# Where the keys of the second attention are split and stacked, in a two-layer gated kernel

## What is computed

```python
# layer 0, attention: 16 heads of 8 channels
q, k, v = Wq @ norm(x) + bq, Wk @ c + bk, Wv @ c + bv
x = x + tanh(g0) * (Wo @ softmax(q k / sqrt(8)) v + bo)
# layer 0, experts: sigmoid gate, 4 of 32 experts (groups of 4, 4 of 8 groups), up -> relu^2 -> down, and a shared one
# layer 1, attention: 8 heads of 16 channels, without projections: q = norm(x), k = v = c
x = x + tanh(g1) * gamma * (softmax(q k / sqrt(16)) v)
# layer 1, experts: softmax gate, 2 of 8 experts, silu(gate) * up -> down, and a shared one
```

## Time and profile before

| what | value |
|---|---|
| median of 3 runs | 777.53 us (777.05 to 778.8) |
| the profiled execution | 779.62 us |
| its span in the profile | 777.4 us |
| TensorE busy | 667.8 us (86%) |
| VectorE busy | 531.6 us (68%) |
| ScalarE busy | 379.0 us (49%) |
| GpSimd busy | 324.1 us (42%) |
| mean granted clock of TensorE | 0.955 |

### The profile page before, as it was taken

The page is one execution under the profiler, slowest core; times in us unless marked ns, Lnnn a source line. Parts: engine busy times, 40 slices in busy tenths (PEclk is TensorE's granted clock), DMA queues, the critical chain, the costliest instruction groups (busy, mean ns, idle before and its releaser), DMA issues.

```text
span 777.4 us, 13620 instructions
## 1 busy us (share of the span) xinstructions
PE 667.8 (86%) x4737; PEld 349.5 (45%) x4738; DVE 531.6 (68%) x1252; ACT 379.0 (49%) x630; POOL 324.1 (42%) x337
## 2 busy tenths in 40 slices
PE   3889999999999899688735788999977999888996
PEld 1233333333333367576402244444433476555763
DVE  3889888888895699155278899997736743222336
ACT  2057888878787344244314566676502213333320
POOL 3535353535011101753568878831100057666530
PEclk9999999999999999889956999999979999999999
DMA  6834343444311800446447778896530022222137
GB/s 164 176 92 122 97 113 96 135 140 130 106 33 38 265 13 2 121 138 184 125 116 190 185 185 205 209 217 158 140 110 28 1 57 83 72 75 66 56 97 258
DMA packets 106362, 93.23 MB, mean 120 GB/s; under 512 B 25205, under 2 KB 92954, under 8 KB 106104
## 3 DMA queue, kind: packets, MB, share of 16 engines
q1 hardware_dynamic: 93600, 67.67, 32.5%
q0 software_dynamic: 8352, 18.74, 8.9%
q10 hardware_dynamic: 4344, 5.97, 2.9%
HBM read 50.63 MB, written 16.01 MB: 86 GB/s over the span
## 4 chain that ended last, share of the span: by engine, by line
PE 56%; DVE 13%; issue 11%; POOL 9%; DMA 4%; ACT 2%; SPq 2%; another core or an unknown queue 1%; ACTq 0%; POOLq 0%; DVEq 0%
PE O L447 9%; PE S L404 9%; PE ST L1547 6%; POOL spare L268 6%; DVE mx L566 4%; PE ST L1473 2%; PE S L1564 2%; PE M L1564 2%; PE ST L943 2%; POOL QKc L279 2%; PE ST L412 2%; PE M L496 2%; DMA QS<-mxT 2%; SPq L165 2%; PE M L489 1%
## 5 line engine op out<-in xcount | busy, mean ns | idle before, releaser
L566 DVE TENSOR_REDUCE mx<-S 128x2 f32<-128x512 f32 x384 | 250.7, 684 | 35.8 <-PE S L404 33.9
L319 ACT ACTIVATE PX<-ST 128x1024 f32<-128x1024 f32 x192 | 195.8, 1022 | 88.2 <-PE ST L412 79.2
L404 PE MATMUL S<-QS 62*128 62x256 bf16 (+1 forms) x768 | 151.2, 292 | 41.6 <-DVE mx L566 28.4
L412 PE MATMUL ST<-QS 64*128 64x256 bf16 (+1 forms) x768 | 141.0, 278 | 7.3 <-DMA QS<-mxT 7.3
L447 PE MATMUL O<-PX,VA 128*32 128x256 f32 x1536 | 123.3, 394 | 0.1
L404 PEld LDWEIGHTS S<-QS 62*128 62x128 bf16 (+1 forms) x768 | 48.7, 97 | 158.2 <-DVE mx L566 95.7
L268 POOL DMA_INDIRECT spare<-ye,GI x64 | 68.9, 1077 | 30.4 <-DMA ye<-QKc 16.1
L1658 POOL DMA_INDIRECT PX<-xn,TI x39 | 39.9, 1022 | 63.4 <-DVE K1n L1847 39.7
L412 PEld LDWEIGHTS ST<-QS 64*128 64x128 bf16 (+1 forms) x768 | 53.4, 96 | 23.3 <-DMA QS<-mxT 9.8
L1547 PE MATMUL ST<-EGU,Cb 128*128 x156 | 54.2, 471 | 6.3 <-ACT Cb L1615 4.9
L786 POOL DMA_INDIRECT PX<-xn,TI x32 | 33.5, 1046 | 61.2 <-DVE spare L1183 44.1
(11 more groups left out here) (302 smaller groups left out, 1114.2 us busy)
## 6 DMA issues: line engine op xcount, KB each, us to landing
QS<-QKs SPq DMA_DIRECT2D x177, 128.0 KB
EGU<-in_ew SPq DMA_DIRECT2D x16, 256.0 KB, 2.8
xn<-spare SPq DMA_DIRECT2D x8, 512.0 KB, 5.7
ye<-QKc SPq DMA_DIRECT2D x32, 128.0 KB
VA<-in_val SPq DMA_DIRECT2D x16, 256.0 KB
spare<-yt SPq DMA_DIRECT2D x16, 256.0 KB, 6.3
Cb<-in_ctx SPq DMA_DIRECT2D x31, 128.0 KB
on<-OS SPq DMA_DIRECT2D x27, 128.0 KB
```

The source lines that it names most:

```text
L319: e.activation(M["PX"][pair % 4][:, :], M["ST"][pair % 2][:, :], ACT.Exp, scale=A.scale).then_inc(A.exp, 1)
L404: got = e.matmul(M["S"][n % 2][:, 256 * a:256 * a + 256], QS[:, 0, 128 * a:128 * a + 128], QS[:, 1, :], start=True, stop=True)
L412: got = e.matmul(M["ST"][(NP * t + k // 2) % 2][:, 512 * u + 256 * a:512 * u + 256 * a + 256], QS[:, 1, 128 * a:128 * a + 128], QS[:, 0, : ...
L566: e.tensor_reduce(M["mx"][b % 2][:, :, A.row_of_max(head)], M["S"][n % 2][:, :].rearrange("p (a s) -> p a s", a=2), AX.X, ALU.max, negate= ...
```

## The change

- In the first attention, GpSimd splits one batch of the context at the end of each step, for batch t+2 in step t (`keys`, four instructions 128 x 256, from `Cb` into `KP`, two buffers in turn). SyncE stores the parts of batch t+1 at the end of step t in DRAM, in the order in which a stack has them (`keys_stored`, six DMAs of 64 KB into `keys_d`). The load of the next context into a buffer waits for its keys also.
- After the experts' normed rows have been stored, SyncE writes zeros and ones into the two hole rows of all 16 batches in `keys_d` (two DMAs from DRAM to DRAM, 1,024 KB each). The routing waits for the stores of the keys, since `KP` lies in its scratch memory.
- The key half of a stack is then loaded by one DMA of 512 KB (`keys_loaded`), with 4 KB for each partition. For that the stacks of the second attention have another order (`QSL1`: all queries, then all keys). Batches 0 and 1 are loaded after experts 23 and 27, with the query halves of their holes (64 KB x 2 each); batches 2 and 3 after the shared expert's last hidden rows, which is now ahead of SyncE's part of the barrier; the others each in step t for batch t+3, ahead of its spreads, in place of `context_load`.
- In the second attention the split and the six spreads have the query alone: 128 x 256 instructions on ScalarE, GpSimd and VectorE, 64 KB for each spread. ScalarE's copy of the context (L362) is gone, and so are `keys_part`, `keys_left`, `keys_spread`, `spread_half` and the four context loads beside the experts.

```diff
 def spread(e, A, M, b, k):
-    QS, parts = M["QS"][A.stack(b)], M["QKs"][b % 2][:, :, :, :].rearrange("p k s t -> p (k s) t")
+    QS, parts = M["QS" + A.name][A.stack(b)], M["QKs"][b % 2][:, :, :, :].rearrange("p k s t -> p (k s) t")
     i, j = TERMS[k]
-    if not A.first and b < A.helped:
-        spread_half(e, A, M, b, k, 0)
+    if not A.first:
+        e.dma_start(QS[k:121 + k:8, :, 0, :], M["QKs"][b % 2][:, i, 0, :]).then_inc(A.sp[b % 2], 16)
         return
...
+def keys_stored(e, w, A, M, b):
+    w.wait_ge(A.keys, 4 * (b + 1))
+    rows = M["keys_d"][b].rearrange("(i k) (g t) -> i g k t", k=8, g=8)
+    for k in range(6):
+        e.dma_start(rows[:, :, k, :], M["KW"][b % 2][:, TERMS[k][1], :]).then_inc(A.kept[b % 2], 16)
+
+def keys_loaded(e, A, M, b):
+    lo = 2048 * A.stack(b) + 1024
+    e.dma_start(M["QSall"][:, lo:lo + 1024], M["keys_d"][b]).then_inc(A.ldc[b % U], 16)
 # attention_sp
+        if A.first and within(b0) and b0 >= U:
...
+            w.wait_ge(A.keys, 4 * (b0 - U + 1))
+            context_load(e, A, M, b0)
...
         if within(b1):
-            w.wait_ge(A.res2, A.k0 + b1 + 1)
+            if not A.first and b1 >= U:
+
+                w.wait_ge(A.st, A.NP * (b1 - U + 1))
+                keys_loaded(e, A, M, b1)
+            w.wait_ge(A.res2, b1 + 1)
...
+        if A.first and within(t + 1):
+            keys_stored(e, w, A, M, t + 1)
 # attention_pool, in every step of the first attention
+    def keys(b):
+        C, K, r = M["Cb"][b % U], M["KP"][b % 2], M["KR"]
+        w.wait_ge(A.ldc[b % U], 16 * (b // U + 1))
+        w.wait_ge(A.kept[b % 2], 96 * (b // 2))
+        w.wait_ge(A.keys, 4 * b)
+        e.tensor_copy(K[:, 0, :], C[:, :]).then_inc(A.keys, 1)
+        w.wait_ge(A.keys, 4 * b + 1)
+        e.tensor_tensor(r, C[:, :], K[:, 0, :], ALU.subtract).then_inc(A.keys, 1)
+        w.wait_ge(A.keys, 4 * b + 2)
+        e.tensor_copy(K[:, 1, :], r).then_inc(A.keys, 1)
+        w.wait_ge(A.keys, 4 * b + 3)
+        e.tensor_tensor(K[:, 2, :], r, K[:, 1, :], ALU.subtract).then_inc(A.keys, 1)
...
+        n = 2 if A.first else 1
+        Q, S = M["QKc"][b0 % 2][:, 0:n, :], M["QKs"][b0 % 2][:, :, 0:n, :]
...
+        if A.first and within(t + 2):
+            keys(t + 2)
 # ffn0_sp, beside the routing and the experts
+    for k in (6, 7):
+        e.dma_start(M["keys_d"].rearrange("b (i k) x -> k (b i) x", k=8)[k],
+                    d["hole"][:, 3072:4096].to_broadcast([NB * P // 8, 1024])).then_inc(B.kept[2], 16)
...
-        if 8 <= x < 8 + U:
-            w.wait_ge(G.dn, 3 * GB)
-            context_load(e, B, M, x - 8)
...
-        if x >= PLACES - 4:
-            next(keys, None)
+        if x in (PLACES - 4, PLACES):
+            w.wait_ge(G.ed, x)
+            stack_ready((x - PLACES + 4) // 4)
+
+    w.wait_ge(G.up, 4 * NGRP)
+    for b in (2, 3):
+        stack_ready(b)
```

More of the change, by code:

```diff
@@ L60, with __init__ @@
 class Layer:
-    def __init__(self, name, H, R, sem, before=None, gathers=None):
+    def __init__(self, name, H, R, sem, before=None, gathers=None, keys=None, kept=None):
         self.name, self.first, self.H, self.R = name, name == "L0", H, R
@@ L76, in __init__ @@
         self.rs, self.res1, self.res2 = (one(w) for w in ("rs", "res1", "res2"))
+        self.keys, self.kept = keys, kept
         self.kc, self.cut0, self.cut1, self.mt, self.exp, self.oe = (
-            one(w) for w in ("kc", "cut0", "cut1", "mt", "exp", "oe"))
+            one(w) if w != "kc" or self.first else None for w in ("kc", "cut0", "cut1", "mt", "exp", "oe"))
         self.sc, self.mtT, self.st, self.pv, self.rb, self.pm = (
@@ L256, in attention_pool @@
                                 ALU.subtract, ALU.mult).then_inc(A.xn, 1)
-        split = within(b0) and not b0 < A.helped
+        split = within(b0) and b0 >= A.aided
         if split and A.first:
@@ L727, in ffn0_sp, with stack_ready @@
         e.dma_start(rows[:, GB * g:GB * g + GB, 0:T], M["XN"][:, GB * g:GB * g + GB, :]).then_inc(G.row, 16)
+    for k in (6, 7):
+        e.dma_start(M["keys_d"].rearrange("b (i k) x -> k (b i) x", k=8)[k],
+                    d["hole"][:, 3072:4096].to_broadcast([NB * P // 8, 1024])).then_inc(B.kept[2], 16)
     w.wait_ge(G.dve, G.at["wd"])
     e.dma_start(rows[:, :, T:ROW0], M["wd"]).then_inc(G.wrow, 16)
-    keys = keys_spread(e, w, G, B, M, d, 0)
+    def stack_ready(b):
+        for k in range(2):
+            w.wait_ge(B.kept[k], 96 * NB // 2)
+        w.wait_ge(B.kept[2], 32)
+        keys_loaded(e, B, M, b)
+        for got in holes(e, M, d, B.stack(b), second=True):
+            got.then_inc(G.late, 16)
     for x in range(E0):
@@ L1052, in ffn0_act @@
             e.activation(M["EH"][y % 2], BK[3 + y % 2][:, 0:P], ACT.Relu).then_inc(G.er, 1)
-        if x >= PLACES + 1:
-            next(keys, None)
-    for _ in keys:
-        pass
 class Steps:
@@ L1084, in marks_dve @@
     w.wait_ge(G.sig, 1 if hi <= 8 else 2)
+    for k in range(2):
+        w.wait_ge(G.again[k], G.again0[k])
     step(e.tensor_tensor(sb, sc, M["bc"][:, :].unsqueeze(1).to_broadcast([P, N, E0]), ALU.add))
@@ L2182, in build @@
         stage = sem("stage")
[L2183 removed]
         X = Routed(sem)
[L2185 removed]
+        keys = sem("keys")
+        L0 = Layer("L0", 16, 8, sem, keys=keys, kept=X.again)
+        L1 = Layer("L1", 8, 16, sem, L0, X.ga, keys, X.again)
         G1 = Sparse(sem, X)
```

144 lines of the change are left out of this document (49 added, 95 removed).

## The result

The changed kernel takes 772.27 us (median of 20 runs, 769.64 to 778.4), the one before 778.24 beside it (20 runs): a ratio of 0.9933 [0.9912, 0.9954], 5.2 us less. Forecast were 767.7 and a gain of 9.8: right in direction, inside the range, and too large by 4 to 5 us. The profiled execution took 771.27 us (span 769.5, against 777.4).

What follows compares the result with a forecast made beforehand. Bounds by stage: TensorE in the first attention, GpSimd then VectorE in the second, TensorE after 505 us. Terms -1.1 + 1.5 - 5.9 - 2.3 - 2.0 = -9.8 us took the median 777.53 to 767.7 us; range 760 to 776.

Steps and rivals of the forecast that it cites:

- first attention: First attention: GpSimd's added instructions, SyncE's six stores and their DMA traffic all fit in idle time, cost 0.
- experts' last store: End of experts: without SyncE's half spreads the last output's store comes sooner, 1.1 us gained, bounds 0 and 2.
- handover: Between experts and second attention: new key and hole loads meet batch 0's gathers, 1.5 us lost, bounds 0 and 4.6.
- steps -1 to 3: Second attention, GpSimd sets the pace: half-width subtractions save 1.17 us a step, 5.9 us over five steps.
- steps 4 to 10 in all, forecast as blocking: Second attention, VectorE sets the pace: half-length GpSimd instructions block its sum half as long, 2.3 us gained, bounds 0 and 4.6.
- from step 11 on, shifted rows: Second attention's last steps: TensorE's 7.3 us of waits for shifted rows shrink, 2.0 us gained, bounds 0 and 5.
- The first attention, SyncE: End of each first-attention step: six added issues, 3.8 us, fill SyncE's 3.63 us idle time; cost 0, bounds 0 and 3.
- GpSimd's four instructions and the traffic: First attention: 1.8 us per step in GpSimd's 6.50 us wait, and 1.8 us of all DMA engines per step; cost 0.
- meetings at random: Steps 4 to 10: by the skill's rule, random timing cuts the blocking loss to a quarter; gain 3.4 us.
- first rival: VectorE takes over GpSimd's steps: the five steps give half, blocking nothing; gain of 4 us, 773.5 us; chance 0.11.
- The burst: 1,280 KB of loads at the handover, 4.6 us of all DMA engines; priced at 1.5 us lost.
- The slower rival: SyncE becomes the first attention's pace if store issues exceed 0.85 us; at 1.05 us, 784.7 us; chance 0.08.

Runs made afterwards that it cites:

- a0: The changed kernel itself, run again in another group: 768.64 us, ratio 0.9878 to the kernel before.
- a1: The changed kernel itself, run once more in another group: 744.64 us, ratio 0.9941 to the kernel before.
- e3: Kernel before, GpSimd's two second-attention subtractions at half width (256 columns), key parts left out: 746.18 us, ratio 0.9974.
- e1: Changed kernel, SyncE issuing the next context load ahead of the six key stores: 738.46 us, ratio 0.988.
- e2: Changed kernel, GpSimd's two second-attention subtractions back at the full width of 512 columns: 763.0 us, ratio 1.0173.
- the two floors: Steps 4 to 10 with GpSimd's subtractions cut to 8 of 256 columns from step 4: 57.59 us in the changed kernel, 58.14 in the kernel before.
- e14: Changed kernel, GpSimd subtracting only 8 of 256 columns from step 4 of the second attention on: 742.39 us, ratio 0.9894.
- e16: Changed kernel, key stores behind the next context's load, run again beside the changed kernel: 742.1 us, ratio 0.9901.
- e9: Changed kernel, key stores behind the next context's load and VectorE's three sums of gathered rows two heads later in steps 0 to 10: ratio 0.9901.
- e8: Changed kernel, VectorE's three sums of gathered rows two heads later in steps 0 to 10: ratio 0.9931.
- e12: Changed kernel, all gathers ahead of GpSimd's subtractions from step 4 on, and key stores behind the next context's load: ratio 0.9939.
- e11: Changed kernel, all of a step's gathers ahead of both GpSimd subtractions from step 4 on: ratio 1.0015.

## Why the prediction was right in direction and too large

| term | predicted | first profile | mean of three profiles |
|---|---|---|---|
| first attention | 0 (0 to +3) | +2.2 | +1.6 |
| experts' last store | -1.1 | not seen, spread of 2.8 in a group | not seen |
| handover | +1.5 | +0.7 by step -1 | +1.1 |
| steps -1 to 3 | -5.9 | -7.5 | -6.0 |
| steps 4 to 10 in all, forecast as blocking | -2.3 | -1.1 | -1.55 |
| from step 11 on, shifted rows | -2.0 | -0.6 | -0.6 |
| sum | -9.8 | -6.3 | -5.4 |

The three profiles are those of the changed kernel (the first, a0, a1), always against the one profile of the kernel before. The time by the ratios is -5.2 in the first group, -9.5 and -4.4 in the other two; the profile of a0 doesn't show what its group gained more. That the sums come near -5.2 is in part luck, since steps -1 to 3 alone differ by 3.5 us between profiles. What failed without doubt are three terms: 4.3 us were forecast for all that lies behind step 4, and 1.7 to 2.7 came (2.1 on average), and 0.9 to 2.2 us (1.6 on average) were lost in a stage for which nothing was forecast.

**Steps -1 to 3** were read right: GpSimd was the pace, and the gain there went with the width. The subtractions take 0.71 and 0.76 us, above the 0.59 forecast, so that the two got 0.94 us shorter per step (from 2.33 to 1.39) and not 1.17. The gain is 1.5 us per step in the first profile and 1.4 in e3, which changes the width alone; with the two other profiles of the changed kernel (0.8 and 1.3) it is 1.2 on average, as forecast. That the average meets the 1.17 is partly luck; what gave more than 0.94 was not settled.

**The first attention, SyncE** is the first failed step. "What is queued behind is the next batch's spreads" was wrong: the next instruction of SyncE's queue is the load of a later batch's context. The 3.63 us of idle time stand behind that load (142.73 in the earlier trace rows), and the stores were put ahead of it. The load stood in the diff, with one wait more. The loss is 0.9 to 2.2 us in the three profiles (2.2 in the mean of the eleven runs that store first), and e1 takes it away. The other terms of this stage, GpSimd's four instructions and the traffic, cost nothing, as forecast.

**The blocking** is the second. "A GpSimd instruction half as long should block half as long" was a term of size alone. What a subtraction costs VectorE goes by whether it meets a sum, and by how many it meets. In e3 the halved subtractions cost the sums more (0.974 + 0.610 us) than the long ones of the kernel before (0.947 + 0.365), and in e2 full width costs 9.4 us more than in the kernel before. "ScalarE's copy and half of its roundings save nothing here" hid the same thing. In steps 9 and 10 the rounding that is 0.21 us shorter brings the subtractions onto both sums, for 0.58 us a step. The copy isn't the cause in those steps, as e3 keeps it and its rounding starts at the same 2.93 us; what sets the start in the earlier steps isn't shown. The size of the term was off at its start too: the 0.65 us per step come from a mean over 420 to 520 us, which takes in steps of GpSimd's pace, and in the seven steps it is 0.947 - 0.41 = 0.54. Halving took the two-sum case from 70.23 to 59.78, and most of that was needed to make good what the new order lost. In place of 2.3 us the blocking gave 0.5 in the first profile (2.7 less 2.2, against the two floors) and at most 1.6 in the others. The rule of the Trainium skill (SBUF — State Buffer, Who interferes with whom) that the prediction weighed was weighed there with meetings at random, which was my assumption and not the page's: -3.4 in place of -2.3, farther off, since in this kernel the meetings repeat in every step. That it is instructions with two inputs in SBUF that are blocked, the runs bear out: with subtractions of 0.26 us (e14) the two sums fall to 0.36 and 0.43, and the reductions out of PSUM have 0.68 in every run.

**The shifted rows** are the third. The 7.3 us of TensorE's waits were put in the last steps and priced at 2.0. Only 0.9 of them lie there, and that stretch, from step 11 to the attention's last reciprocal, got 0.6 us shorter (45.48 to 44.86). 5.4 lay in steps 4 to 10, where VectorE sets the pace, and taking 3.3 away gave at most 0.5.

One sum of the prediction is off as well, without weight: for its first rival, half of the five steps and no blocking give -1.1 + 1.5 - 3.0 - 2.0 = -4.6, not -4.

**The burst** was priced well at its own place (+1.1 against +1.5). The first gather started at 375.20 us and not near 374. The slower rival, SyncE as the pace of the first attention, had the right engine and the wrong mechanism: its issues, 0.63 to 0.85 us in the first profile, stay within the 0.85 from which it decides, and yet some 2 us were lost through one load behind them.

No version is shown to be the best, but the stores belong behind the next context's load: e1 and e16 take 0.988 and 0.990 of the kernel before. In the pairs that differ in this alone, the ratios give a gain of 3.0 us (e16 against a1), 2.3 (e9 against e8) and 5.9 (e12 against e11), each with wide intervals.

## What to carry to other kernels

When a wait or a row of issues is put at the end of a loop's turn in one queue, read what stands at the head of the next turn: a load two steps ahead counts, even if nobody waits for it in the timeline of before. Price blocking between two engines by where their instructions meet in a steady step, from the timeline, and not by mean length; a change that only shortens a third engine's instruction by 0.2 us can move the meeting. And a wait that lies in a stretch where another engine has no gap is worth little until that engine has one: 0.5 us at most for 3.3 here.

## What the runs showed of the hardware

A sum of VectorE with both inputs in SBUF can be stretched beyond the whole length of the GpSimd instruction that it meets, even if its recorded start is earlier: 1.87 us against 0.41 undisturbed, beside a subtraction of 1.17 that started 0.40 us after it (e2). It ends some 0.3 us after that one. It can also go the other way. Where the sum's recorded start comes 0.05 to 0.08 us after the subtraction's, the sum keeps its 0.36 us and the subtraction is stretched: 1.42 and 1.43 us for 1.16 (steps 7 and 10 of the kernel before), 0.96 for 0.67 (e3). So the recorded starts don't tell which of the two has to wait.

The same program takes 53 to 56 us for its experts in some groups and 63 to 67 in others, with 238 to 242 and 252 to 259 us for the rest; the first attention, with the load ahead of the stores, differs by 0.03 us between them. What the slower groups lack was not settled.
